# Delta-rule attention with a gated feed-forward on one core: two of four output products moved between the products with the inverse, the inverse stored packed, the next rows normed in halves, four spans to a loop iteration

## The chip, the cores and the metric

One core of a Trainium2 chip. The metric is the device time of one launch in microseconds (us), the median of several runs. PE is TensorE (matmuls), DVE is VectorE, ACT is ScalarE, POOL is GpSimd, SP issues the DMAs. Each engine has its own instruction stream and they meet only at semaphores.

## The reference

For x of shape [2, 4096, 512], in float32:

```
xn = layernorm(x)
q, k = l2norm(heads(xn @ Wq)) / sqrt(32), l2norm(heads(xn @ Wk))       16 heads of 32
v = heads(silu(xn @ Wv));  beta = sigmoid(xn @ Wb)
per head, for each token t:  S += k_t (beta_t (v_t - S^T k_t))^T ;  o_t = S^T q_t
attn = rmsnorm(o) * o_norm_weight @ Wo
ffn = (silu(xn @ fp8(gate_w) * gate_scale) * (xn @ fp8(up_w) * up_scale)) @ fp8(down_w) * down_scale
out = x + attn + ffn
```

## The kernel before

A span is 256 tokens of each of the two batch rows, 512 token rows in four tiles of 128. The 16 spans run one after another, since the states S (a 32 by 32 matrix for each batch row and head) pass from one to the next. `two_spans(it)` on each engine holds two of them (`for par in range(2)`). It is written out once for the first two spans and once as the body of a loop (`Fori(1, SPANS // 2)`, lines 503 to 505), which comes round again before spans 4, 6, 8, 10, 12 and 14, counted from 0: six times. The order on each engine is written by hand, and semaphores count upwards over the whole program.

One span, on PE:

- Thirteen projections (`project`, line 380) of 12 matmuls each, 8 for beta. A factor is split in two 16-bit parts, so each product is three matmuls. Job numbers (line 25) name them: K, Q, B, V. Between them stand the grams (`gram(g)`, g 0 to 7): for chunks of 32 tokens, k^T k and k^T q, as 32 by 32 products in float32. The profile counts 64 matmuls to a `gram` (each float32 product is two).
- Four output products (`project_out`, line 321), 12 matmuls each, with the o of the span before. Its parts `o_hi` and `o_lo` lie in the last four slots of `f_hi` and `f_lo`. DVE adds the results to the residual `xs` (`add_out`, line 1049).
- 24 gate and up products (`gate_up`, lines 390 and 391), 8 matmuls each. ACT takes silu (`silu_gate`), DVE multiplies (`fuse_tile`, line 1013), and each of the 12 tiles is split (`high_part` on ACT, `low_part` on DVE, line 1003).
- Eight groups of products with the inverse (lines 441 to 452; 64 matmuls each in the profile, written `T<-kpv,mt`). Their stationary operand is `tt`, in the memory of `mt`: the transposed inverse of a unit triangular 32 by 32 matrix for each chunk and head. DVE and ACT read the results (`read_w`, line 1042; `copy_u`, line 605).
- The chain over 8 chunks (lines 473 to 501): two blocks of 64 small matmuls a chunk with DVE steps between them (lines 1093 to 1115). In the waits stand pieces of the four down products (`down`, lines 461 and 462) and the transposes of the next span's rows (`transpose_xn`, line 311).

DVE computes the inverse by forward substitution, 62 dependent operations (`row_products`, `off_rows`, lines 1020 and 1027), and does other work between them at places given by tables (lines 43 to 46): `V_AT`, `OUT_AT`, `VK_AT`, `FUSE_AT`, each an operation number to an index. `t_transposed(s)` (line 1037) stores a half of the result transposed into `tt`, with 32 elements of 4 bytes between neighbours it writes:

```
tt = mt[:, :].rearrange("p (n t) -> p n t", t=CHUNK)
nc.vector.transpose(tt[:, 32 * s:32 * s + 32, :].rearrange("p n t -> p t n"), t_prob[:, s])
```

The inverse can start once both halves of the grams are read (`read_grams(s)`, lines 956 to 963). The first four groups of products wait for `tt_ready` of half 0, the last four for half 1.

The next span's rows: SP loads both batch rows when y of the span before last is stored, and that waits for all four `add_out`. DVE takes the statistics of four tiles (line 744) between the last `read_w`, aggregates (line 1103) in chunk 0 of the chain, POOL takes the root (line 726), DVE applies (line 747) in chunks 1 and 2, and PE transposes in chunks 2 to 5. POOL also clears the matrix `at` (line 717), runs the Newton steps for the norms (line 683) and adds the down products (`add_down`, line 732).

## Time and profile before

| | before |
|---|---|
| median of 3 runs | 2594.55 us (2590.03 to 2601.16) |
| the profiled execution, its own time | 2598.04 us |
| its span, first to last instruction | 2596.3 us |
| PE busy | 2290.9 us, 88% |
| DVE busy | 1932.2 us, 74% |
| ACT busy | 661.6 us, 25% |
| POOL busy | 315.2 us, 12% |
| granted PE clock, mean | 0.980 |
| DMA | 54.56 MB, of it 5.47 MB instructions on queue 8 |

In the page a row of a timeline gives the start, the duration, the engine, the line, the operation with its tiles, how many were merged, and in brackets how long the engine had been idle before it and what ended that. "issue" there means that nothing in the profile held the engine. A dense matmul of 512 columns shows 0.38 us, but they follow one another every 0.216 us. One span of the 16 lasts some 152 us.

### The profile page before, as it was taken

The numbers are of one execution on the slowest core, as the hardware profiler recorded it, in microseconds if no ns is written. First come the engines' busy times: TensorE is split into PE (matmuls) and PEld (weight loads), VectorE is DVE, ScalarE is ACT, GpSimd is POOL, SyncE is SP. The second block draws the span as 40 slices with busy tenths as digits, with TensorE's granted clock in tenths as the row PEclk, the third lists the DMA queues.
The fourth block names the chain that finished last, engine by engine and source line by source line (L and its number), as shares of the span: only waits on it lengthen the run. The fifth ranks groups of instructions, "written<-read, shape, count | busy, mean of one in ns | idle before, by whom it ended". The sixth has DMA issues, their size and how long they took to land.

```text
span 2596.3 us, 92717 instructions
## 1 busy us (share of the span) xinstructions
PE 2290.9 (88%) x40736; PEld 1286.9 (50%) x40992; DVE 1932.2 (74%) x3291; ACT 661.6 (25%) x1110; POOL 315.2 (12%) x528
## 2 busy tenths in 40 slices
PE   0198999989899998989989899998989899898996
PEld 0045545455554545455454555545554454545543
DVE  7986685958768596776959587695967769496785
ACT  2123222213222222222222222222222222122221
POOL 4510101001010100102010010201001020100200
PEclk9999999999999999999999999999999999999998
DMA  5100010000001000000000000010100100000010
GB/s 170 61 18 2 3 34 4 33 3 19 18 3 34 3 34 3 17 20 3 34 4 34 3 13 24 3 34 3 34 3 3 34 3 34 4 34 3 2 34 18
DMA packets 27184, 54.56 MB, mean 21 GB/s; under 512 B 5152, under 2 KB 5152, under 8 KB 26784
## 3 DMA queue, kind: packets, MB, share of 16 engines
q1 hardware_dynamic: 26784, 48.55, 5.5%
q8 instruction: 334, 5.47, 0.9%
q14 instruction: 66, 0.54, 0.1%
HBM read 31.76 MB, written 16.78 MB: 19 GB/s over the span
## 4 chain that ended last, share of the span: by engine, by line
PE 88%; issue 6%; DVE 4%; DMA 0%; ACT 0%; POOL 0%; SPq 0%; DVEq 0%
PE D L380 21%; PE T L306 21%; PE D L391 13%; PE D L390 13%; PE D L462 8%; PE D L321 7%; PE D L461 4%; PE D L311 1%; DVE kq L227 1%; DVE at L781 0%; DVE f_lo L780 0%; DVE w_lo L822 0%; DVE stats L744 0%; DVE wgu L233 0%; DVE kq L1042 0%
## 5 line engine op out<-in xcount | busy, mean ns | idle before, releaser
L390 PE MATMUL D<-xt_hi,wgu 128*128 128x512 f16 x1536 | 582.1, 379 | 0.0
L391 PE MATMUL D<-xt_lo,wgu 128*128 128x512 f16 x1536 | 582.1, 379 | 0.0
L462 PE MATMUL D<-wd,f_lo 128*128 128x512 bf16 x768 | 297.0, 387 | 43.1 <-issue 43.1
L380 PE MATMUL D<-xt_hi,w_hi 128*128 128x512 f16 x832 | 319.3, 384 | 12.9 <-issue 12.9
L380 PE MATMUL D<-xt_lo,w_hi 128*128 128x512 f16 x832 | 318.4, 383 | 0.0
L380 PE MATMUL D<-xt_hi,w_lo 128*128 128x512 f16 x768 | 293.9, 383 | 0.0
L598 ACT ACTIVATE sg<-D,gs 128x512 f32<-128x512 f32 x192 | 132.0, 687 | 573.6 <-PE D L391 573.6
L1027 DVE TENSOR_TENSOR at<-at,outer_v 128x62 f32<-128x62 f32 (+15 forms) x496 | 259.3, 523 | 12.1
L1020 DVE TENSOR_TENSOR outer_v<-mt,at 128x62 f32<-128x62 f32 (+15 forms) x496 | 258.2, 521 | 11.6
L391 PEld LDWEIGHTS D<-xt_lo,wgu 128*128 128x128 f16 x1536 | 150.3, 98 | 181.2
L390 PEld LDWEIGHTS D<-xt_hi,wgu 128*128 128x128 f16 x1536 | 150.3, 98 | 181.2
L1113 DVE STREAM_TRANSPOSE outer_p<-T 128x256 f32<-128x256 f32 x128 | 57.6, 450 | 193.4 <-PE T L306 193.4
L461 PE MATMUL D<-wd,f_hi 128*128 128x512 bf16 x512 | 198.2, 387 | 0.0
L306 PE MATMUL T<-kpv,mt 32*32 32x64 f32 x8192 | 136.3, 222 | 67.5 <-issue 67.5
L306 PE MATMUL T<-kq,state 32*32 32x64 f32 x8192 | 155.3, 221 | 24.7 <-ACT kpv L605 18.9
L306 PEld LDWEIGHTS T<-kq,state 32*32 32x32 f32 x8192 | 130.0, 108 | 79.0 <-issue 78.7
L306 PEld LDWEIGHTS T<-kpv,mt 32*32 32x32 f32 x8192 | 126.7, 110 | 81.0 <-issue 81.0
L726 POOL TENSOR_TENSOR rstd<-var_e,neg_half 128x4 f32<-128x4 f32 x16 | 16.4, 1026 | 1222.9 <-DVE var_e L1105 1222.9
L1093 DVE STREAM_TRANSPOSE outer_v<-T 128x256 f32<-128x256 f32 x128 | 57.6, 450 | 143.0 <-PE T L306 143.0
L306 PE MATMUL T<-kpv 32*32 32x64 f32 x8192 | 148.2, 219 | 3.4 <-issue 2.7
L732 POOL TENSOR_TENSOR xs<-xs,fuse 128x512 f32<-128x512 f32 x64 | 81.1, 1267 | 575.8 <-DVE fuse L1087 575.8
L306 PEld LDWEIGHTS T<-kpv 32*32 32x32 f32 x8192 | 125.4, 107 | 46.1 <-issue 45.9
(153 smaller groups left out, 3314.0 us busy)
## 6 DMA issues: line engine op xcount, KB each, us to landing
xs<-_attn_hidden_states_dram SPq DMA_DIRECT2D x34, 512.0 KB, 4.2
out_dram<-xs SPq DMA_DIRECT2D x32, 512.0 KB, 3.3
f_hi<-in_L_ffn_down_w_dram SPq DMA_DIRECT2D x4, 768.0 KB, 4.5
kq<-in_L_ffn_gate_w_dram SPq DMA_DIRECT2D x3, 768.0 KB, 4.4
f_hi<-in_L_ffn_up_w_dram SPq DMA_DIRECT2D x2, 768.0 KB, 6.2
kq<-in_L_ffn_up_w_dram SPq DMA_DIRECT2D x2, 768.0 KB, 6.6
qt<-in_L_attn_Wq_dram SPq DMA_DIRECT2D x1, 1024.0 KB, 8.1
kpv<-in_L_attn_Wk_dram SPq DMA_DIRECT2D x1, 1024.0 KB, 10.4
```

The costliest lines, as they stand in the source:

```text
L306: last = nc.tensor.matmul(out[s], lhs[s], rhs[s], start=start, stop=True, skip_group_check=shared)
L321: ins = nc.tensor.matmul(D[bank][:, :], o_part[:, m, j * P:(j + 1) * P], w[:, m, :], start=n == 0, stop=n == 3 * MS - 1)
L380: last = nc.tensor.matmul(D[bank][:, :], w[:, k, cols], xp[:, k, :], start=n == 0, stop=n == len(parts) * KT_ - 1)
L390: nc.tensor.matmul(D[bank][:, :], wgu[:, k, c:c + P], xt_hi[:, k, :], start=k == 0, stop=False)
L391: last = nc.tensor.matmul(D[bank][:, :], wgu[:, k, c:c + P], xt_lo[:, k, :], start=False, stop=k == KT_ - 1)
L461: nc.tensor.matmul(D[bank][:, :], f_hi[:, ic, j * P:(j + 1) * P], wd[:, ic, :], start=ic == 0, stop=False)
L462: last = nc.tensor.matmul(D[bank][:, :], f_lo[:, ic, j * P:(j + 1) * P], wd[:, ic, :], start=False, stop=ic == IC - 1)
L598: nc.scalar.activation(sg[:, ic % 2, :], D[bank_of(gate_up_job(2 * ic))][:, :], ACT.Silu, scale=gs[:, ic:ic + 1]).then_inc(sg_ready, 1)
L732: nc.gpsimd.tensor_tensor(xs[:, par, j, :], xs[:, par, j, :], fuse[:, j % 2, :], ALU.add).then_inc(acc_ready, 1)
L1020: solved[0] = step(nc.vector.tensor_tensor(products(j), m_prob[:, :, j, j + 1:].unsqueeze(3).to_broadcast(shape), t_prob[:, :, j, 0:j + 1] ...
L1027: solved[0] = step(nc.vector.tensor_tensor(rest, rest, products(j), ALU.subtract))
L1093: nc.vector.transpose(blocks(outer_v), chain_banks(c)[:, :, :, 0, :]).then_inc(ws_read, 1)
```

## The change

- PE: output products 0 and 1 stay ahead of the gate and up products. Products 2 and 3 are cut in halves of 6 matmuls, and one half follows every second of the eight groups with the inverse. A gram pair is separated by a projection, and four matmuls of job 9 stand ahead of grams 6 and 7. The beta projection comes sixth instead of third.
- The inverse's transpose is packed: DVE writes it contiguously, and PE reads its stationary operand with a step of 32 elements.
- o: DVE writes the normed o into `at`, and the two 16-bit parts lie in the memory of `qt`. The last span's parts stay in `f_hi` and `f_lo`. POOL clears `at` after `o_low` instead of at the span's start, so writing beta on the diagonal became a step of its own (`set_diagonal`).
- DVE: all 12 `fuse_tile` stand between the operations of the inverse; `add_out` 2 and 3 follow during the products with the inverse.
- Rows of the next span: each batch row is loaded, measured, aggregated and applied by itself, with a semaphore each.
- Loops: `some_spans(it)` holds four spans, written out once and looped three times, so it comes round twice.

```diff
+TURNS = 4
-JOB_K, JOB_B, JOB_Q, JOB_V, JOB_WO, JOB_GU, JOB_DN = (0, 3, 5, 7), 2, (1, 4, 6, 8), (9, 10, 11, 12), 13, 17, 41
+JOB_K, JOB_B, JOB_Q, JOB_V, JOB_WO, JOB_GU, JOB_DN = (0, 2, 4, 7), 5, (1, 3, 6, 8), (9, 10, 11, 12), (13, 14, 39, 40), 15, 41
-XT_AT = {2: 0, 3: 1, 4: 2, 5: 3}
+XT_AT = {2: 0, 3: 1, 5: 2, 6: 3}
-V_AT = {0: 0, 4: 1, 9: 2, 13: 3}
-OUT_AT = {17: 0, 20: 1, 22: 2, 25: 3}
-VK_AT = 23
-FUSE_AT = {27: 0, 31: 1, 34: 2, 37: 3, 40: 4, 43: 5, 46: 6, 50: 7, 54: 8, 60: 9}
+V_AT = {0: 0, 2: 1, 7: 2, 12: 3}
+OUT_AT = {16: 0, 18: 1}
+VK_AT = 18
+FUSE_AT = {20: 0, 24: 1, 27: 2, 30: 3, 33: 4, 36: 5, 39: 6, 42: 7, 45: 8, 49: 9, 53: 10, 58: 11}
+STATS_AT, AGGREGATE_AT, APPLY_AT = {2: 1}, {0: 0, 3: 1}, {1: 0, 4: 1}
...
-        tt = mt[:, :].rearrange("p (n t) -> p n t", t=CHUNK)
+        tt = mt[:, :].rearrange("p (g t n) -> p g t n", g=2, t=CHUNK)
-        o_hi, o_lo = f_hi[:, IC - MS:, :], f_lo[:, IC - MS:, :]
+        o_half = o_wide.bitcast(F16)
+        o_hi, o_lo = (o_half[:, i * MS * TOK:(i + 1) * MS * TOK].rearrange("p (m n) -> p m n", m=MS) for i in range(2))
+        last_hi, last_lo = f_hi[:, IC - MS:, :], f_lo[:, IC - MS:, :]
+        o_normed = at[:, :]
...
-                    sp.wait_ge(wo_added, at_span(it, par, TILES, 2 * TILES))
...
+                    for b in range(BATCH):
+                        sp.wait_ge(wo_added, at_span(it, par, TILES, TILES + 2 * b + 2, turns=2))
+                        sp.nop(nofuse=True)
+                        store_y(it * 2 + par, par, b)
+                        sp.wait_ge(y_stored, at_span(it, par, 32, 16 * b + 16, turns=2))
+                        sp.nop(nofuse=True)
+                        load_x(it * 2 + (par + 2), par, b)
...
-                    project(8)
                     gram(4)
                     gram(5)
+                    project(8)
+                    project(9, end=4)
                     gram(6)
                     gram(7)
-                    for job in range(9, PROJECTIONS):
+                    project(9, first=4)
+                    for job in range(10, PROJECTIONS):
                         project(job)
 
                     pe.wait_ge(olo_ready, since(1, 1))
-                    for j in range(TILES):
-                        project_out(j, take(JOB_WO + j))
+                    for j in range(2):
+                        project_out(j, take(JOB_WO[j]))
...
-                            last = quads(T[g % 4][:, 64 * n:64 * n + 64], tt[:, pc, :], kpv[:, 1:3, pc * DH:(pc + 1) * DH])
+                            last = quads(T[g % 4][:, 64 * n:64 * n + 64], tt[:, pc // 32, :, pc % 32], kpv[:, 1:3, pc * DH:(pc + 1) * DH])
                         last.then_inc(tiled_done, 1)
+                        if g % 2:
+                            j, half = 2 + g // 4, g // 2 % 2
+                            bank = bank_of(JOB_WO[j]) if half else take(JOB_WO[j])
+                            project_out(j, bank, groups=range(2 * half, 2 * half + 2))
...
-            with pe.Fori(1, SPANS // 2) as it:
-                two_spans(it)
+            with pe.Fori(1, SPANS // TURNS) as it:
+                some_spans(it)
...
-                    pool.wait_ge(xt_lo_ready, since(TILES, TILES))
+                    o_norm(it, turn, step, after_last)
+                    pool.wait_ge(olo_ready, since(1, 1))
                     pool.nop(nofuse=True)
                     nc.gpsimd.memset(t_flat, 0.0).then_inc(zero_ready, 1)
-                    o_norm(it, par, step, after_last)
...
-                        nc.vector.transpose(tt[:, 32 * s:32 * s + 32, :].rearrange("p n t -> p t n"), t_prob[:, s]).then_inc(tt_ready, 1)
+                        nc.vector.transpose(tt[:, s], t_prob[:, s]).then_inc(tt_ready, 1)
...
                     t_transposed(0)
-                    fuse_tile(10)
                     t_transposed(1)
-                    fuse_tile(11)
-
-                    dve.wait_ge(x_loaded, since(32, 64))
-                    dve.nop(nofuse=True)
+
                     for g in range(8):
                         read_w(g)
                         if g == 1:
                             low_part(IC - 1)
-                        if g > 3:
-                            step(layer_norm_stats(g - 4, 1 - par))
+                        if g == 4:
+                            add_out(2)
+                    read_statistics(0)
+                    add_out(3)
...
+                        if c in AGGREGATE_AT:
+                            aggregate(AGGREGATE_AT[c])
+                        if c in APPLY_AT:
+                            apply_norm(APPLY_AT[c])
...
+                        if c in STATS_AT:
+                            read_statistics(STATS_AT[c])
```

New functions on DVE: `read_statistics(b)` waits for `x_loaded[b]` and takes the statistics of tiles 2b and 2b+1, `aggregate(b)` and `apply_norm(b)` do the rest for them.

How the instructions of PE move, at the products with the inverse. Before, first the last gate and up products, then all eight groups (256 products are 512 matmuls in the profile), then the chain:

```order
L390 MATMUL D<-xt_hi,wgu 128x512
L391 MATMUL D<-xt_lo,wgu 128x512
L306 MATMUL T<-kpv,mt 32x64 x256
L306 MATMUL T<-kq,state 32x64 x32
L461 MATMUL D<-wd,f_hi 128x512
L462 MATMUL D<-wd,f_lo 128x512
```

The same place with the change (the line of `quads` is now 314, that of `project_out` 329):

```order
L401 MATMUL D<-xt_lo,wgu 128x512
L314 MATMUL T<-kpv,mt 32x64 x64
L329 MATMUL D<-wo_hi,qt 128x512 x2
L329 MATMUL D<-wo_lo,qt 128x512
L329 MATMUL D<-wo_hi,qt 128x512 x2
L329 MATMUL D<-wo_lo,qt 128x512
L314 MATMUL T<-kpv,mt 32x64 x64
L329 MATMUL D<-wo_hi,qt 128x512 x2
L329 MATMUL D<-wo_lo,qt 128x512
```

Six dense matmuls now follow every two groups, 24 in all, and they are gone from the place ahead of the gate and up products.

On DVE, the end of the inverse before. Line 1037 is `t_transposed`, 1003 and 1013 are `low_part` and `fuse_tile`:

```order
L1020 TENSOR_TENSOR outer_v<-mt,at 128x62
L1027 TENSOR_TENSOR at<-at,outer_v 128x2x31
L1037 STREAM_TRANSPOSE mt<-at 128x32x32
L1003 TENSOR_TENSOR f_lo<-fuse,f_hi 128x512
L1013 SCALAR_TENSOR_TENSOR fuse<-D,usf,sg 128x512
L1037 STREAM_TRANSPOSE mt<-at 128x32x32
L1003 TENSOR_TENSOR f_lo<-fuse,f_hi 128x512
L1013 SCALAR_TENSOR_TENSOR fuse<-D,usf,sg 128x512
L1042 STREAM_TRANSPOSE kq<-T 128x8x32 x2
```

And with the change (1071 is `t_transposed`, 1076 `read_w`, 1083 `add_out`, 765 the statistics):

```order
L1054 TENSOR_TENSOR outer_v<-mt,at 128x62
L1061 TENSOR_TENSOR at<-at,outer_v 128x2x31
L1071 STREAM_TRANSPOSE mt<-at 128x1024 x2
L1076 STREAM_TRANSPOSE kq<-T 128x8x32 x2
L1037 TENSOR_TENSOR f_lo<-fuse,f_hi 128x512
L1076 STREAM_TRANSPOSE kq<-T 128x8x32 x3
L1083 SCALAR_TENSOR_TENSOR xs<-D,w_inv,xs 128x512
L1076 STREAM_TRANSPOSE kq<-T 128x8x32 x3
L765 BN_STATS stats<-xs 128x6 x2
L1083 SCALAR_TENSOR_TENSOR xs<-D,w_inv,xs 128x512
```

Both transposes follow the inverse at once and write 1024 elements in a row; tiles 10 and 11 have moved ahead of them, output adds 2 and 3 behind.

## Rows read from the trace of the kernel before

**Rows 1.** The page, part 4: the chain of work that ended last, by engine.
```profile
PE 88%; issue 6%; DVE 4%; DMA 0%; ACT 0%; POOL 0%; SPq 0%; DVEq 0%
```
**Rows 2.** Windows, span 6: length; PE, PEld, DVE, ACT, POOL busy; clock; DMA.
```profile
1086.00:1138.00 52.00, 52.00 (x243) 23.52 (x241) 49.52 (x80) 14.69 (x24) 0.00 (x0) 1.00 0.13 41
1138.00:1153.00 15.00, 10.09 (x527) 9.19 (x528) 8.03 (x16) 3.58 (x9) 0.00 (x0) 0.89 0.02 5
1153.00:1196.00 43.00, 38.72 (x1120) 25.36 (x1128) 21.42 (x48) 5.57 (x13) 4.82 (x4) 1.00 0.01 3
```
**Rows 3.** Groups of PE over the run: busy, mean ns, idle before and its releaser.
```profile
L380 PE MATMUL D<-xt_hi,w_hi 128*128 128x512 f16 x832 | 319.3, 384 | 12.9 <-issue 12.9
...
L306 PE MATMUL T<-kpv,mt 32*32 32x64 f32 x8192 | 136.3, 222 | 67.5 <-issue 67.5
...
L306 PE MATMUL T<-kq 32*32 32x64 f32 x8192 | 129.5, 215 | 19.9 <-issue 19.9
```
**Rows 4.** Timeline of PE, span 4: products with the inverse, then the chain's start.
```profile
832.42 2.56 PE L306 MATMUL T<-kpv,mt 32*32 32x64 f32 x168
836.60 1.98 PE L306 MATMUL T<-kpv,mt 32*32 32x64 f32 x126 [1.62 <-issue]
840.53 1.98 PE L306 MATMUL T<-kpv,mt 32*32 32x64 f32 x126 [1.95 <-issue]
...
847.23 2.33 PE L306 MATMUL T<-kq,state 32*32 32x64 f32 x64 [1.15 <-ACT kpv L605]
```
**Rows 5.** Timeline of PE, span 6, at the same place.
```profile
1138.26 2.56 PE L306 MATMUL T<-kpv,mt 32*32 32x64 f32 x168
...
1146.10 3.59 PE L306 MATMUL T<-kpv,mt 32*32 32x64 f32 x126 [1.95 <-issue]
...
1152.83 0.71 PE L306 MATMUL T<-kq,state 32*32 32x64 f32 x34 [1.19 <-ACT kpv L605]
```
**Rows 6.** Timeline of PE, span 7, at the same place.
```profile
1290.31 3.88 PE L306 MATMUL T<-kpv,mt 32*32 32x64 f32 x261
...
1302.71 0.21 PE L306 MATMUL T<-kq,state 32*32 32x64 f32 x1 [1.20 <-ACT kpv L605]
```
**Rows 7.** Timeline of PE: first matmul of span 6, some after; one of span 10.
```profile
1042.59 0.39 PE L380 MATMUL D<-xt_hi,w_hi 128*128 128x512 f16 x1 [2.16 <-issue]
...
1044.05 0.63 PE L380 MATMUL D<-xt_hi,w_hi 128*128 128x512 f16 x1
1044.47 0.63 PE L380 MATMUL D<-xt_lo,w_hi 128*128 128x512 f16 x1
...
1652.53 0.63 PE L380 MATMUL D<-xt_hi,w_hi 128*128 128x512 f16 x1
```
**Rows 8.** Timeline of PE, span 6: grams 4 to 7.
```profile
1075.20 0.87 PE L306 MATMUL T<-kq 32*32 32x64 f32 x46 [1.11 <-issue]
```
**Rows 9.** Timeline of DVE, span 6: from the grams' reading to the inverse's transposes.
```profile
1076.12 1.25 DVE L956 STREAM_TRANSPOSE mt<-T 128x1024 f32<-128x1024 f32 x1 [2.17 <-PE T L306]
...
1089.42 0.74 DVE L1049 SCALAR_TENSOR_TENSOR xs<-D,w_inv,xs 128x512 f32<-128x512 f32 x1
1090.08 0.58 DVE L1027 TENSOR_TENSOR at<-at,outer_v 128x414 f32<-128x414 f32 x1
...
1133.39 1.98 DVE L1037 STREAM_TRANSPOSE mt<-at 128x1024 f32<-128x1024 f32 x1
1135.22 0.67 DVE L1003 TENSOR_TENSOR f_lo<-fuse,f_hi 128x512 f16<-128x512 f32 x1
...
1136.46 1.94 DVE L1037 STREAM_TRANSPOSE mt<-at 128x1024 f32<-128x1024 f32 x1
```
**Rows 10.** Timeline of DVE, span 6: a step of the chain in chunk 3.
```profile
1170.68 0.45 DVE L1093 STREAM_TRANSPOSE outer_v<-T 128x256 f32<-128x256 f32 x1 [0.32 <-PE T L306]
```
**Rows 11.** Timeline of SP, span 6: y stored, x loaded.
```profile
1100.02 0.97 SPq L279 DMA_DIRECT2D out_dram<-xs  x2
1105.55 0.97 SPq L275 DMA_DIRECT2D xs<-_attn_hidden_states_dram  x2
```

233 lines of the change are left out of this document (124 added, 109 removed).

## The prediction

> **What bounds the kernel now.** I read the chain of work that ended last first: PE holds 88% of it and time without a releaser 6% [rows 1]. So PE's own stream sets the end, and a change is worth what it takes out of that stream, or out of its gaps. Next the windows of one span in the middle of the run [rows 2]. In the dense middle (52 us) PE is busy all the time and DVE for 49.5 us. In the chain (43 us) PE is busy for 38.7. In the 15 us with the products of the inverse PE is busy for only 10.1, and its clock is 0.89. The groups of PE say what these holes are [rows 3]: 67.5 us in all before the products with the inverse, 19.9 us before the grams, 12.9 us before first projections, nearly all under "issue", with no semaphore named.
>
> The timeline shows what they look like [rows 4]. From 832.42 us 168 small matmuls run in 2.56 us, then PE stands still, then come 126 in 1.98 us, and again. The blocks begin at 836.60 and 840.53, 3.93 us apart, and 126 matmuls with their weight loads are 252 instructions. I read this as the instruction stream: small matmuls use instructions faster than they arrive, some 256 per 3.9 us. Dense matmuls need 2 instructions per 0.216 us, seven times fewer than arrive. So a small matmul stage is worth filling with dense work, and that is what the change does. The products with the inverse last 14.8 us in span 4, 14.6 in span 6, 12.4 in span 7, from first product to the chain's start [rows 4 to 6].
>
> **The change, part by part.** Costs are per middle span; 15 spans count, since the first is set by its setup as well.
>
> Loop: PE stands still 12.9 us in six first projections [rows 3], 2.16 us in one of them [rows 7]; these are the six times when the loop comes round. Two remain, four go: 4 × 2.15 = 8.6 us. After that stop the matmuls of span 6 follow each other every 0.42 us, with durations of 0.63, a clock of half speed, for 8 matmuls: 1.7 us more. Three of the six loop heads show it (spans 6, 10 and 14 [rows 7]), so of four removed I take off two: 3.4 us.
>
> Grams: the stop of 1.11 us [rows 8], 19.9 / 16 = 1.2 us a span [rows 3], goes, since a projection and four more matmuls now stand between. Those four matmuls are ahead of gram 7 instead of behind it: 4 × 0.216 = 0.9 us later. Of the 0.3 us left I count 0.2, since a little of the stop may stay: 3.0 us over 15 spans.
>
> Start of the products with the inverse. This is the term on which most depends, since PE and DVE are now equally long here. From DVE's reading of gram 7 (1076.12) PE reaches the products at 1138.26, after 62.1 us, and DVE has the first transposed half at 1133.39 + 1.98 = 1135.37, after 59.3 [rows 5, 9]. PE loses two output products (24 × 0.216 = 5.2 us) and the four matmuls from that stretch and would arrive after 56.1. DVE: two output adds go behind, 0.66 us each from start to start [rows 9], 1.3; the first transpose becomes contiguous, and for it I take the other transpose of 1024 elements, 1.25 us [rows 9], so 0.7 less; tiles 10 and 11 come ahead of it, each with its low part 1.24 us (1135.22 to 1136.46 [rows 9]), 2.5 more; and of the 2.5 us that DVE is idle in this stretch, waiting for PE [rows 2], I count 0.5 as gone. That gives 59.3 − 1.3 − 0.7 + 2.5 − 0.5 = 59.3. With the semaphore's way of 0.3 us PE starts after 59.6, 2.5 us earlier than before, not 5.2 + 0.9. DVE becomes the bound of this stretch, and PE waits about 3.5 us in a place where it never waited: −2.5 × 15 = −37.5 us.
>
> Length of that stage. Its work is 512 × 0.0140 us (2.56 less a tail of 0.2, over 168 [rows 4]) = 7.2, plus 24 × 0.216 = 5.2, plus some 1.0 for eight changes between small and dense, plus the 1.2 us for ACT's last copy [rows 4]: 14.6 us if instructions never lack. By instructions: 1024 + 48 less the 336 of the first block is 2.9 blocks of 3.93 us, behind a first arrival after 4.2 us: the last block arrives after 12 us and takes 1 to 3 more. Work and arrivals don't overlap perfectly. Before it was 13.9 us on average over rows 4 to 6; I take 15.6, so +1.7 × 15 = +25.5 us. Lower end: 13.9, nothing more; upper end 18, if both delays add. The Trainium skill (Runtime: NRT & Kernel Launch, Instruction fetch mechanics) holds that crossing from one block of instructions to the next is mostly hidden. By that the stage would take its 14.6 us of work, the sum would be 15 us lower; the stops of 1.62 and 1.95 us per 252 instructions [rows 4] contradict it, and they decide.
>
> Clock there. In span 6 126 matmuls take 3.59 us instead of 1.98 [rows 5], so half speed also comes after stops of 1.4 to 1.9 us. It then costs little, since instructions were lacking anyway. Now PE is idle for 3.5 us before the stage, and work fills the stage: 3.4 us at half speed would cost up to 1.7. I take +0.4 × 15 = +6 us; ends 0 and +1.7 a span.
>
> Chain. Statistics of the second batch row (2 × 0.65 us) come in chunk 2, beside a low part and a down product's reading, before DVE's step of chunk 3, for which DVE had only 0.32 us to wait [rows 10]. So that step is about 0.9 us late, and PE has a down piece and one transpose (0.5) less to cover it: +0.2 a span, +3 us. In return chunk 0 and 2 lose the aggregation and one apply, which were covered.
>
> At nothing I cost: tanh behind the o copy on ACT (busy 25%); POOL's clearing, 1.8 us, now after `o_low`, which has several us of grams and sums on DVE before `set_diagonal`; the beta projection's place; o's parts in `qt` (same sizes). Loads: the second row's store can start only after output add 3, now at the chain's start instead of at 1099.8. From there store and load took 1100.02 to some 1111 us, 11 us [rows 11]. The statistics of that row come some 16 us into the chain, so it is covered with 4 to 5 us to spare.
>
> Sum: −8.6 − 3.4 − 3.0 − 37.5 + 25.5 + 6 + 3 = −18.0 us. On the profiled execution, 2598.0, that is 2580.0; it was 3.5 us above the median of the runs, so I expect a median of 2576.6 us.
>
> **The rivals.**
>
> A, the gain is whole. Instructions arrive in time and the clock stays up: stage +0, clock +0. −8.6 − 3.4 − 3.0 − 37.5 + 3 = −49.5, so 2545 us. For it: the dense pieces give each pair of groups 1.3 us in which hardly an instruction is used. Against: 3.9 us per 256 instructions remains, and 1072 are needed.
>
> B, nothing is gained in the spans. If the write step is not what makes the transposes take 1.98 us, they stay, +0.7 a span, and the stage comes to 15.9: per span −2.5 + 0.7 + 2.0 + 0.4 + 0.2 − 0.2 = +0.6, so +9 against −12 for the loops: 2592 us. Against: the other 1024-element transpose takes 1.25 us [rows 9] though it reads with a step. The change then doesn't do what it says.
>
> C, slower: the packed inverse moves the step from DVE's write to PE's weight load, which now reads 32 elements 128 bytes apart. No row has such a load. From below the price is zero, if loads stay behind the matmuls before them. From above it is DVE's: (1.98 − 1.25) / 1024 = 0.7 ns per element, 23 ns per load of 32. Four row groups load side by side, 64 × 2 loads follow one another in each: 3.0 us a span, in a stage now filled with work: −18 + 45 − 3 = +24, so 2619 us. It decides from about 16 ns a load on (2.1 us a span, which turns −18 into +13). For it: small matmuls at half clock take twice the time (3.59 against 1.98 us [rows 5]), so the array and not the issue sets their pace, and a slower load may show. Against: for half of each pair the array streams 64 columns, behind which a load can hide. The Trainium skill (Advanced Engine Details and Errata, SBUF Cachelines) speaks against the change here: lines are 16 bytes, and a new line with each access costs. By that the transposes get faster and the loads slower, as the 1.98 against 1.25 us bears out for DVE.
>
> D, slower: PE's idle 3.5 us puts every stage at half speed for some 6.8 us, twice as long as in rows 5. Its work is then 3.4 us longer, of which lacking instructions hide some 0.8: +2.6 a span for the +0.4, so −18 + 2.2 × 15 = +15, 2610 us. It decides from 2.5 us a span on.
>
> **How the numbers follow.** About 0.5%, 13 us, is what a measurement can tell. Chances: my forecast 0.34, A 0.15, B 0.26, C 0.16, D 0.09. Faster by over 0.5% (below 2581.6): forecast and A, 0.49. Within: B, 0.26. Slower (over 2607.5): C and D, 0.25. Range: from below A, with the stage's start a further 0.3 us earlier a span, 2540, up to C with a little of D, 2624. My own case alone: 2562 to 2590.
>
> **What would show it.** PE's group of first projections waits 2 times, some 4 us. The grams' 19.9 us nearly vanish. Before the first product with the inverse PE is idle some 3 to 4 us, released by DVE's transpose: right for the start term. That transpose takes 1.2 to 1.3 us: else B. A group of 64 of these products takes clearly over 1.1 us at full clock: C. The output matmuls between them show 0.63 us: D. Stage from first product to the chain some 15.6 us. If PE is not idle before it, or the stage takes as long as before, my two largest terms are wrong.

## The result: slower by a third of a per cent, and the profile after

| | before | after |
|---|---|---|
| median of the runs, us | 2594.21 (18 runs, 2588.11 to 2604.66) | 2602.31 (18 runs, 2596.98 to 2609.03) |
| ratio | | 1.0033, 95% interval 1.0023 to 1.0044 |
| span of the profiled execution, us | 2596.3 | 2600.4 |

The forecast was 2576.6 us. The time lies in its range and within 0.5% of before, but the change moved it the other way. The change cost some 8 us.

All times below that are given by span come from the timeline of PE, cut at five points of each span: first projection, first output product, end of the last gate/up product, first product with the inverse, start of the chain. Summed over the 16 spans, after against before (in brackets what one span takes, before and after; for the stage the mean of spans 1 to 14):

| part of the span | after less before, us |
|---|---|
| projections and grams | +2.8 |
| output products, gate and up | −82.9 (51.8, then 46.6) |
| PE's wait ahead of the products with the inverse | +67.1 (0.1, then 4.1 to 4.4) |
| stage of the products with the inverse | +34.3 (13.70, then 16.04) |
| chain, and the gap to the next span | −17.4 |
| sum | +3.9 |

The two profiled executions differ by 4.1 us, so the table holds nearly all of it. Span 0 is an exception in the stage: it took 19.2 us there before and 15.6 after.

First the windows of span 12 of the changed kernel, cut at its own edges; they answer to [rows 2]. Columns: length, busy time of PE, weight loads, DVE, ACT and POOL, the granted clock, the share and rate of the DMAs.

```profile
1996.00:2047.60 51.60, 51.60 (x240) 23.29 (x238) 48.87 (x84) 16.60 (x27) 0.00 (x0) 1.00 0.06 21
2047.60:2052.00 4.40, 0.20 (x5) 0.06 (x5) 4.11 (x9) 0.63 (x1) 0.00 (x0) 0.91 0.00 0
2052.00:2067.70 15.70, 14.97 (x536) 10.94 (x536) 6.63 (x13) 3.07 (x8) 0.00 (x0) 0.92 0.02 4
2067.70:2110.00 42.30, 40.62 (x1134) 25.20 (x1134) 23.00 (x51) 5.08 (x11) 5.18 (x5) 1.00 0.09 28
```

There is a row that before did not have: 4.4 us in which PE does next to nothing and DVE works. In the stage behind it PE is busy for 14.97 of 15.70 us, where it was busy for 10.09 of 15.00. The filling worked; the 4.2 us ahead of it ate what it brought.

The groups of PE answer to [rows 3], with the weight loads of the same products:

```profile
L390 PE MATMUL D<-xt_hi,w_hi 128*128 128x512 f16 x832 | 319.5, 384 | 6.3 <-issue 6.3
...
L314 PE MATMUL T<-kpv,mt 32*32 32x64 f32 x8192 | 159.9, 238 | 69.1 <-DVE mt L1071 50.4 <-issue 18.3
L314 PE MATMUL T<-kq 32*32 32x64 f32 x8192 | 131.9, 215 | 16.1 <-issue 15.3 <-ACT kq L575 0.8
...
L314 PEld LDWEIGHTS T<-kpv,mt 32*32 32x32 f32 x8192 | 148.9, 141 | 99.0 <-issue 98.7
```

The idle time ahead of the products with the inverse is as large as before (69.1 against 67.5 us), but another kind. It was stops inside the stage. Now 50.4 us are one wait of 4.2 us for DVE's transpose of the inverse (L1071), named in 12 spans; in the other four the same wait stands under "issue". The grams' stops have not gone, 16.1 against 19.9 us.

The timeline of PE in span 12 answers to [rows 4 to 6]: the products with the inverse between the output products (one row is kept of each of those), and the chain's first group.

```profile
2051.97 3.25 PE L314 MATMUL T<-kpv,mt 32*32 32x64 f32 x128 [4.20 <-DVE mt L1071]
2055.15 0.61 PE L329 MATMUL D<-wo_hi,qt 128*128 128x512 f16 x2
...
2056.55 2.10 PE L314 MATMUL T<-kpv,mt 32*32 32x64 f32 x128
...
2059.97 2.08 PE L314 MATMUL T<-kpv,mt 32*32 32x64 f32 x128
...
2063.39 2.09 PE L314 MATMUL T<-kpv,mt 32*32 32x64 f32 x128
...
2067.71 1.10 PE L314 MATMUL T<-kq,state 32*32 32x64 f32 x64
```

128 small products take 2.1 us at full clock, and 3.25 us behind the wait (3.06 to 3.64 over the 16 spans). Only one stop of 0.73 us is left inside this stage, and the chain starts without the 1.15 us for ACT's copy [rows 4].

DVE in the same place answers to [rows 9]: its last gated tile, the last two rows of the inverse, and both transposes in one row.

```profile
2047.96 0.69 DVE L1037 TENSOR_TENSOR f_lo<-fuse,f_hi 128x512 f16<-128x512 f32 x1
2048.57 0.74 DVE L1047 SCALAR_TENSOR_TENSOR fuse<-D,usf,sg 128x512 f32<-128x512 f32 x1
...
2050.12 0.22 DVE L1061 TENSOR_TENSOR at<-at,outer_v 128x62 f32<-128x62 f32 x1
2050.38 2.37 DVE L1071 STREAM_TRANSPOSE mt<-at 128x1024 f32<-128x1024 f32 x2
```

Two transposes in 2.37 us: the step in the write was indeed what made each take 1.98. But PE is kept waiting until 2051.97.

What DVE itself waits for shows in the chain of work that ended last (start, duration, engine and line), from PE's last gate/up product to the products with the inverse; the stretches under "issue" and the inverse's rows between are left out:

```profile
2047.56 0.23 PE D L401
...
2047.96 0.10 DVE f_lo L1037
...
2048.57 0.74 DVE fuse L1047
...
2050.38 1.26 DVE mt L1071
2051.63 0.34 issue
2051.97 3.25 PE T L314 x128
```

The chain runs along PE to its last gate/up product and only there goes over to DVE: that product belongs to tile 11, and `fuse_tile(11)` waits for it even ahead of tile 10's low part. In all 16 spans DVE starts this low part 0.42 or 0.57 us after the start of that product, after 0.15 us of idling; then follow 2.41 us for the low part, the tile and four operations of the inverse, 1.25 for the transpose and 0.21 or 0.35 of way. That is 4.28 or 4.58 us from the product's start, and explains why the wait hardly varies.

And the grams of span 10, which answer to [rows 8]:

```profile
1675.28 1.88 PE L314 MATMUL T<-kq 32*32 32x64 f32 x118
1678.41 0.38 PE L314 MATMUL T<-kq 32*32 32x64 f32 x10 [1.25 <-issue]
...
1682.28 1.65 PE L314 MATMUL T<-kq 32*32 32x64 f32 x100
1686.10 1.06 PE L314 MATMUL T<-kq 32*32 32x64 f32 x28 [2.17 <-issue]
...
1687.50 0.63 PE L390 MATMUL D<-xt_hi,w_lo 128*128 128x512 f16 x1
```

One stop of 1.1 us had become two, 3.4 us together, with half clock behind them (0.63 us for a projection matmul instead of 0.38). I ask below whether such stops stand where PE's stream of instructions passes from one block of 256 to the next; I call that place an edge. Spans 0, 1, 6, 10 and 14 look like this and take 44.9 to 46.9 us from the first projection to the first output product. The other eleven take 40.9 to 42.6, where before took 42.0 to 43.8 in its spans 1 to 15.

### The profile page after: what moved, and what is told of

Its sections match the earlier page's. It is cut to its first block, busy times and chain, and to the rows that moved or that the text cites. A ratio compares the mean times of both kernels' runs of the same rounds, so it can differ in the third digit from the quotient of the medians.

```text
span 2600.4 us, 92532 instructions
## 1 busy us (share of the span) xinstructions
PE 2354.5 (91%) x40992; PEld 1294.3 (50%) x40992; DVE 1918.8 (74%) x3307; ACT 663.9 (26%) x1110; POOL 325.7 (13%) x544
## 4 chain that ended last, share of the span: by engine, by line
PE 89%; DVE 7%; issue 3%; DMA 0%; POOL 0%; ACT 0%; DVEq 0%; SPq 0%
PE T L314 22%; PE D L390 21%; PE D L401 13%; PE D L400 13%; PE D L329 7%; PE D L477 7%; PE D L478 6%; PE D L319 1%; DVE kq L232 1%; DVE mt L1071 1%; DVE kpv L1154 0%; DVE at L803 0%; DVE f_lo L802 0%; DVE state L1163 0%; DVE w_lo L844 0%
## 5 line engine op out<-in xcount | busy, mean ns | idle before, releaser
L477 PE MATMUL D<-wd,f_hi 128*128 128x512 bf16 x768 | 293.7, 382 | 1.5 <-issue 1.4
L478 PE MATMUL D<-wd,f_lo 128*128 128x512 bf16 x768 | 291.1, 379 | 0.0
L314 PE MATMUL T<-kpv,mt 32*32 32x64 f32 x8192 | 159.9, 238 | 69.1 <-DVE mt L1071 50.4
L748 POOL TENSOR_TENSOR rstd<-var_e,neg_half 128x2 f32<-128x2 f32 x32 | 22.6, 706 | 1486.2 <-DVE var_e L1099 1486.2
L314 PEld LDWEIGHTS T<-kpv,mt 32*32 32x32 f32 x8192 | 148.9, 141 | 99.0 <-issue 98.7
L1076 DVE STREAM_TRANSPOSE kq<-T 128x256 f32<-128x256 f32 x128 | 57.4, 448 | 153.2 <-PE T L314 153.1
L329 PE MATMUL D<-wo_hi,qt 128*128 128x512 f16 x512 | 159.0, 392 | 1.3 <-issue 1.2
L314 PEld LDWEIGHTS T<-kq,state 32*32 32x32 f32 x8192 | 123.4, 105 | 67.3 <-issue 67.2
L314 PE MATMUL T<-kq,state 32*32 32x64 f32 x8192 | 148.0, 216 | 8.2 <-issue 5.1
L314 PEld LDWEIGHTS T<-kpv 32*32 32x32 f32 x8192 | 122.8, 105 | 50.7 <-issue 50.5
```

What stands on the lines that cost most here:

```text
L314: last = nc.tensor.matmul(out[s], lhs[s], rhs[s], start=start, stop=True, skip_group_check=shared)
L329: ins = nc.tensor.matmul(D[bank][:, :], o_part[:, m, j * P:(j + 1) * P], w[:, m, :], start=m == 0 and n == 0, stop=m == MS - 1 and n == 2)
L477: nc.tensor.matmul(D[bank][:, :], f_hi[:, ic, j * P:(j + 1) * P], wd[:, ic, :], start=ic == 0, stop=False)
L478: last = nc.tensor.matmul(D[bank][:, :], f_lo[:, ic, j * P:(j + 1) * P], wd[:, ic, :], start=False, stop=ic == IC - 1)
L1076: nc.vector.transpose(kq[:, 8 * g:8 * g + 8, 0, :], T[g % 4][:, :].rearrange("p (n a d) -> p n a d", n=8, a=2)[:, :, 0, :]).then_inc(w_rea ...
```

## The experiments

Ratios are to runs of before on the same chip, with their 95% intervals. "The changed kernel" is the one above, 1.0033. The traces come from several chips, on which before took 2586.9 to 2594.2 us. Two of them are of the changed kernel with nothing but empty instructions added, and between these three the mean of spans 1 to 14 is 15.96 to 16.17 us for the stage and 42.38 to 42.80 up to the output products: smaller differences than that say nothing.

**Two gated tiles behind the transposes.** If the wait is DVE's, take DVE's work out of its way.

```
-FUSE_AT = {..., 45: 8, 49: 9, 53: 10, 58: 11}
+FUSE_AT = {..., 45: 8, 49: 9}
...
                     t_transposed(0)
+                    fuse_tile(10)
                     t_transposed(1)
+                    fuse_tile(11)
```

> The changed kernel with tiles 10 and 11 of the gated product (each with its low part 1.24 us on DVE) put back behind the first and the second transpose of the inverse, where before had its last tiles. PE waits 4.1 to 4.4 us a span for the first of these transposes. Theory G (DVE's own row of work between the grams and the transposes sets the start of the inverse products): 2.5 us less work stand ahead of the first transpose, so PE's wait falls to about 1.7 us, the stage starts 2.5 us earlier in each span, and, if the stage keeps its 16.0 us, the time falls by 2.5 x 16 = 40 us, to 2562. Rival H (the instruction stream sets the end of the stage, which is where PE's blocks of small products arrive): the wait before the stage shrinks but the stops inside it grow by as much, 16.0 becomes 17.5 to 18.5, and the time falls by 0 to 15 us, 2587 to 2602. Rival I (the low parts are now late for the down products in the chain, or the second group's transpose is late): the stage gets 1.2 us longer by waits for DVE, time 2582.

Measured: 2536.28 us, 0.9803 (0.9782 to 0.9823). PE:

```profile
L314 PE MATMUL T<-kpv,mt 32*32 32x64 f32 x8192 | 143.1, 221 | 33.3 <-DVE mt L1071 17.9 <-issue 14.9
```

Two lines of order on DVE turn a loss of 0.33% into a gain of 2%. G holds and H falls: PE's wait fell from 4.1 to 4.4 us to 1.4 to 1.7, and the stage did not grow but shrank, from 16.04 to 14.82 us on average over spans 1 to 14. The chain of work now goes over from PE to DVE earlier, at tile 9 (at 2000 us in span 12, 8.6 us ahead of the products with the inverse), so tile 11 no longer ties the inverse to PE's last product. The stage starts 3.05 us earlier and is 1.2 us shorter. The second part I had not expected; the products' mean duration fell from 238 to 221 ns, which pointed at the clock. The granted clock in the stage says the same: on average over spans 1 to 14 it was 0.87 in the changed kernel and is 1.00 here. The stage of span 12, against the row above with a clock of 0.92:

```profile
2008.60:2023.80 15.20, 13.89 (x536) 9.91 (x536) 8.99 (x17) 4.11 (x10) 0.00 (x0) 1.00 0.02 5
```

Span 0 goes the other way: its stage takes 22.98 us instead of 15.64. ACT scales the 12 tiles of the down weights once, there, behind its last high part, and its copies of the products wait behind that. With tile 11 later this work starts later, and PE stands still before the third pair of groups:

```profile
222.43 7.44 ACT L632 ACTIVATE wd<-wd,row_inv 128x512 bf16<-128x512 bf16 x12
```

```profile
230.23 2.95 PE L314 MATMUL T<-kpv,mt 32*32 32x64 f32 x99 [4.77 <-issue]
```

All kernels below with tiles 10 and 11 behind the transposes have a long stage in span 0 (19.6 us in the one with all output products in front, 21 to 22 in the others). Against 15 us in the other spans some 6 to 8 us, 0.3%, are left there for an order that scales the weights elsewhere; no run tried it.

**One low part more behind the transpose.** `fuse_tile(9)` no longer starts with tile 8's low part, which now stands ahead of `fuse_tile(10)`.

```
-                            fuse_tile(FUSE_AT[op])
+                            fuse_tile(FUSE_AT[op], low=FUSE_AT[op] != 9)
...
                     t_transposed(0)
+                    low_part(8)
                     fuse_tile(10)
```

> As the kernel that took tiles 10 and 11 behind the transposes of the inverse (0.980 of before), and tile 8's low part (0.6 us on DVE) also goes behind the first transpose instead of ahead of tile 9. PE still waited 1.4 to 1.7 us a span for that transpose. If DVE's row of work is still what sets the start, the wait falls by 0.6 us, and 16 x 0.6 = 10 us come off: 0.976 of before. If the instruction stream now sets the end of the stage, the stage grows by as much, and the ratio stays 0.980.

Measured: 2524.43 us, 0.9769 (0.9742 to 0.9796). The wait fell to 0.7 to 1.1 us, the stage stayed (14.87), and a span lost another 0.85 us, 0.6 of it in the wait. DVE's row of work is still what decides there. The intervals of this ratio and the last overlap; the wait itself does not leave doubt:

```profile
L314 PE MATMUL T<-kpv,mt 32*32 32x64 f32 x8192 | 143.3, 220 | 23.9 <-issue 12.1 <-DVE mt L1071 10.7
```

**The wait filled with matmuls for nothing.** The changed kernel, with

```
                     pe.wait_ge(vk_ready, since(1, 1))
+                    pe.wait_ge(m_ready, since(2, 2))
+                    pe.wait_ge(p_ready, since(2, 2))
+                    for n in range(16):
+                        nc.tensor.matmul(T[0][:, :], wgu[:, 0, 0:P], xt_hi[:, 0, :], start=True, stop=True)
                     for g in range(8):
```

> The changed kernel with 16 matmuls of 128x512, whose result nothing reads, ahead of the first product with the inverse (3.5 us of work in the 4.1 to 4.4 us in which PE waits there). Theory K (the wait before the stage is what lowers the clock at its start, and the low clock makes the stage 16.0 us instead of the 14.8 that it takes in the kernel whose wait is 1.4 to 1.7 us): the clock stays up, the first products take 216 ns and the stage 14.8 to 15.0 us; the stage's mean falls by 1.0 to 1.2 us a span, up to 19 us in all. Rival L (the stage is longer because instructions lack, and the wait has nothing to do with it): the stage stays at 16.0 us or gets longer, since 32 more instructions pass. The 32 instructions a span also move the edges in the grams, so the whole time may differ by some long spans; the stage is read by itself.

Measured: 2588.35 us, 0.9980 (0.9966 to 0.9994), so work that nobody needs makes the changed kernel some 14 us faster. The timeline, the 16 matmuls and the first two groups behind them:

```profile
1425.13 3.62 PE L456 MATMUL T<-xt_hi,wgu 128*128 128x512 f16 x16
1429.30 2.09 PE L314 MATMUL T<-kpv,mt 32*32 32x64 f32 x128 [0.55 <-DVE mt L1075]
...
1432.72 2.09 PE L314 MATMUL T<-kpv,mt 32*32 32x64 f32 x128
```

The start is no earlier (4.0 to 4.2 us from the last gate/up product to the first product with the inverse), but the first 128 products take 2.09 us in every span where they took 3.06 to 3.64, and the stage is 15.06 us on average instead of 16.04, at a granted clock of 1.00 instead of 0.87. K holds. The wait costs twice: itself, and 1 us of low clock behind it. Not all of the gain need be the clock, since the 32 instructions a span also move the stops in the grams.

**The inverse unpacked.** Layout and transposes as before, all else changed.

```
-tt = mt[:, :].rearrange("p (g t n) -> p g t n", g=2, t=CHUNK)
+tt = mt[:, :].rearrange("p (n t) -> p n t", t=CHUNK)
...
-    last = quads(T[g % 4][:, 64 * n:64 * n + 64], tt[:, pc // 32, :, pc % 32], ...)
+    last = quads(T[g % 4][:, 64 * n:64 * n + 64], tt[:, pc, :], ...)
...
-    nc.vector.transpose(tt[:, s], t_prob[:, s])
+    nc.vector.transpose(tt[:, 32 * s:32 * s + 32, :].rearrange("p n t -> p t n"), t_prob[:, s])
```

> The changed kernel with the transposed inverse laid out as before: DVE writes it with a step, PE loads it contiguously. Theory: DVE's two transposes together take 3.9 us again instead of 2.4, 0.7 us later for the first half, so PE's wait before the inverse products is 0.7 us longer, 4.9 us, and the stage starts 0.7 us later; each weight load in it takes 110 ns instead of 141, worth 0.4 us a span in bursts where 128 products take 2.09 us. Net +0.3 to +0.7 a span, 5 to 11 us slower than the changed kernel, 2607 to 2613. Rival C of the prediction in a small form (the strided loads cost more than the bursts show): the stage is 1 us or more shorter, and the time 2595 or less.

Measured: 2608.45 us, 1.0074 (1.0052 to 1.0095), 0.4% or 10.6 us over the changed kernel. DVE, then PE, from the end of the transposes on:

```profile
2056.58 3.67 DVE L1071 STREAM_TRANSPOSE mt<-at 128x1024 f32<-128x1024 f32 x2
```

```profile
2058.84 3.64 PE L314 MATMUL T<-kpv,mt 32*32 32x64 f32 x128 [4.87 <-DVE mt L1071]
...
2064.46 2.00 PE L314 MATMUL T<-kpv,mt 32*32 32x64 f32 x128
```

The wait is 0.66 us longer a span, which is the 10.6 us. At full clock 128 products take 2.00 us with contiguous loads and 2.09 with strided ones: 0.09 × 4 = 0.4 us a span is what the strided loads can cost by these rows, and the stage's mean (16.20 here, 16.04 in the changed kernel) shows nothing of it. Packing is worth what it takes from DVE. The Trainium skill (Advanced Engine Details and Errata, SBUF Cachelines) says that a different 16-byte line with each access costs. That is borne out for DVE, 3.67 against 2.37 us for the two transposes. For PE the weight loads do get longer (141 ns in the changed kernel, 120 here), but nearly all of it lies beside matmuls.

**All output products in front again.** The changed kernel with `project_out` for all four ahead of the gate and up products, and DVE's tables of before (the last two tiles behind the transposes).

```
-JOB_..., JOB_WO, JOB_GU, ... = ..., (13, 14, 39, 40), 15, ...
+JOB_..., JOB_WO, JOB_GU, ... = ..., (13, 14, 15, 16), 17, ...
...
-                    for j in range(2):
+                    for j in range(TILES):
                         project_out(j, take(JOB_WO[j]))
...
-                        if g % 2:
-                            ...
```

> The changed kernel with all four output products ahead of the dense middle again, and DVE's output adds and gated tiles at the places that they had in the kernel before; kept are the packed inverse, four spans to a loop iteration, the norming in halves and the interleaved grams. It tells what the pieces are worth on their own. Before had 52 us of dense middle, no wait, and 13.7 us of inverse products. If the pieces themselves bring nothing but what DVE's order gives back, this kernel has a wait of 0 to 0.5 us, a stage of 13.7, and is some 7 us (loop heads) faster than before: 0.997. Against the kernel with tiles 10 and 11 behind the transposes (0.980) that would make the pieces worth 1.7%, 44 us, or 2.8 us a span out of the 5.2 us of matmuls that they move. If it comes out near 0.985 instead, the pieces are worth little and the gain of that kernel came from the packing and the loop.

Measured: 2598.51 us, 1.0054 (1.0030 to 1.0077). No wait (0.1 us), a stage of 14.53 us, and 0.5% slower than before where I expected 0.3% faster. Without the pieces the loop, the packing, the norming and the interleaved grams together bring nothing, and cost some 14 us. Against the first kernel of this section (0.9803) the pieces are worth 2.5% once DVE's order lets them: the start of the stage is 3.8 us earlier (94.48 against 90.67 from the span's start), and the stage with two output products in it takes 14.82 us against 14.53 without. Of 5.2 us of matmuls moved into the stage, 0.3 us show there. I expected 13.7 us for this stage. The stops inside it are those of before (4.1 us a span in both) and so is the last wait for ACT (1.2); it is the 512 products that are busy for 9.3 us instead of 8.4:

```profile
989.69 2.08 PE L314 MATMUL T<-kpv,mt 32*32 32x64 f32 x126 [1.54 <-issue]
```

126 of them take 2.08 us with strided loads and took 1.98 with contiguous ones [rows 4], 0.4 us for 512. So here, with no dense work between, the strided loads do cost. A granted clock of 0.94 instead of 0.95 gives perhaps 0.2 more; the rest is open.

**Shifting PE's stream.** Two kernels have 24 and 64 empty instructions on PE ahead of the first span.

```
             pe.wait_ge(ffn_ready, 1)
+            for _ in range(24):
+                pe.nop(nofuse=True)
```

> The changed kernel with 24 empty instructions on PE ahead of the first span, so that everything behind them stands 24 places later in PE's stream. Theory E (the stops between grams come where the stream crosses from one block of 256 instructions to the next, and hurt only in those copies of the span in which such an edge falls into grams 4 to 7 at a bad place): the five long spans (0, 1, 6, 10, 14, with 46.5 us from start to the output products where the others have 41.0) change. By my count of the instructions the copies stand at other places and none or one (that of spans 5, 9 and 13) is then bad: the time falls by 5.3 x 5 = 26 us, to 2576, or by 5.3 x 2 = 11, to 2592, if the copy of spans 5, 9, 13 becomes bad. Rival F (the stops belong to the order of the work, for instance to what DVE and ACT do beside the grams): 24 empty instructions, under 1 us once, change nothing; the same five spans are long and the time is 2602.

> The same with 64 empty instructions. Theory E: the copy of spans 5, 9 and 13 then stands where that of spans 6, 10, 14 stood, so spans 5, 9, 13 get the 5.3 us and spans 0, 1, 6, 10, 14 lose them: 2 x 5.3 = 11 us faster than the changed kernel, 2592, and the long spans are others. Rival F: no change in time, and the same spans are long.

Measured: 2596.03 us, 1.0027 (1.0011 to 1.0043), and 2599.36 us, 1.0038 (1.0022 to 1.0055). The same five spans are long. That looks like F, but the trace says more. I numbered all records of PE in it from the start: matmuls, weight loads and the waits and register operations of its sequencer. In the changed kernel the two stops of span 1 stand before numbers 6337 and 6593, those of span 6 before 32193 and 32449: 256 apart each, and 101 × 256 from one span to the other. With 24 or 64 empty instructions ahead all four numbers are the same. The empty instructions themselves leave no record, so the stops stand before the very same matmuls. Either edges don't matter, or empty instructions don't shift them. These two runs decide nothing by themselves.

**The same with real instructions.**

```
                 pe.wait_ge(sq_ready, i + 1)
+                if i == len(SQUARE_ORDER) - 1:
+                    for c in range(32):
+                        nc.tensor.matmul(T[0][:, 200 + c:201 + c], squares[i % 2][:, (c % IC) * P:(c % IC + 1) * P], ones[:, :],
+                                         start=True, stop=True)
```

> The changed kernel with 32 tiny matmuls (128x1, results unused) with their weight loads among those of the setup, 64 recorded instructions ahead of the first span, at once behind its setup. The 24 and 64 empty instructions moved no stop by a single recorded instruction, so they stood nowhere in the stream that the stops count; these do. Theory E (edges of blocks of 256 instructions): counted in recorded instructions, an edge now falls 26 + 64 instructions before and so on in each copy, so that the copy of spans 5, 9 and 13 (gram 4 began 14 instructions past such a place after the shift, as that of span 1 did before it) becomes long, 45 to 47 us up to the output products, and spans 0, 1, 6, 10, 14 short, 41 to 42. Time: 3 long spans for 5, about 2 x 5 = 10 us less than the changed kernel, ratio to before 0.999. Rival F (spans 1, 6, 10, 14 are long for what else happens in them or for the time at which they come): the same spans are long as without the tiny matmuls, ratio 1.003.

Measured: 2592.52 us, 1.0023 (1.0008 to 1.0038). PE's grams 4 to 7, first in span 5, then in span 6:

```profile
905.80 1.88 PE L314 MATMUL T<-kq 32*32 32x64 f32 x119
909.21 0.32 PE L314 MATMUL T<-kq 32*32 32x64 f32 x9 [1.53 <-issue]
...
913.02 1.65 PE L314 MATMUL T<-kq 32*32 32x64 f32 x101
916.57 0.63 PE L314 MATMUL T<-kq 32*32 32x64 f32 x27 [1.90 <-issue]
...
1062.36 2.00 PE L314 MATMUL T<-kq 32*32 32x64 f32 x128
...
1067.84 2.00 PE L314 MATMUL T<-kq 32*32 32x64 f32 x128
```

Theory E holds. 64 recorded instructions in the setup, a microsecond of work, and the two stops of span 6 are gone and stand in span 5, after nearly the same counts (118, 10, 100, 28 in span 10 of the changed kernel; 119, 9, 101, 27 here). Spans 0, 5, 9 and 13 are long now (49.5, 46.6, 44.6 and 44.9 us), spans 1, 6, 10 and 14 take 40.9 to 41.0. The stops stand before numbers with the same remainder by 256 as before the shift (27073 and 6337 both leave 193). In time the gain is small where I expected 10 us: three long spans and a longer span 0 take the place of five, and two of the chains have become long (46.4 and 48.2 us in spans 7 and 11). The interval overlaps that of the changed kernel.

The Trainium skill (Runtime: NRT & Kernel Launch, Instruction fetch mechanics) says that crossing a block's edge is mostly hidden. In dense stretches it is (PE is busy for all of the 51.6 us in the first window above); between two grams that stand 12 or 16 dense matmuls apart, it costs 1.53 and 1.90 us in these rows, and whether it does hangs on where the edge falls.

**The last four grams behind one another.** Projection ahead of gram 4, four matmuls behind gram 7.

```
                     project(7)
+                    project(8)
                     gram(4)
                     gram(5)
-                    project(8)
-                    project(9, end=4)
                     gram(6)
                     gram(7)
-                    project(9, first=4)
-                    for job in range(10, PROJECTIONS):
+                    for job in range(9, PROJECTIONS):
```

> The changed kernel with the last four grams behind one another again, and the projection and the four matmuls that stood between grams 5 and 6 around them (the projection ahead of gram 4, the four matmuls behind gram 7). By the prediction's term for the grams each span gets its stop of 1.1 us back and gram 7 is read some 0.3 us later, +1 us a span, 16 us slower than the changed kernel, 2610 on the scale on which that took 2602. By theory E the interleaving is what makes five spans 4 to 5 us long and saves 1 us in the other eleven: undone, 11 x 1 us are lost and 5 x 3 us are won, and the time is within 5 us of the changed kernel.

Measured: 2589.73 us, 1.0017 (1.0002 to 1.0032), if anything better than the changed kernel. Every fourth span takes 40.8 to 40.9 us up to the output products and nearly all others 42.1 to 42.7; none of spans 1 to 15 is long. Against this the interleaving gives 1.2 to 1.7 us in seven spans and 0.6 in span 0, takes 2.6 to 4.8 in spans 1, 6, 10 and 14, and 0.5 to 1.4 in the other four. With four spans to an iteration it gains nothing, where my term for it was −3 us.

**Dense work spread evenly, in the grams and then in the stage too.** From the second kernel of this section (0.9769):

```
                     gram(4)
+                    project(8, end=6)
                     gram(5)
-                    project(8)
-                    project(9, end=4)
+                    project(8, first=6)
                     gram(6)
+                    project(9, end=4)
                     gram(7)
```

and, in the second of them, besides that:

```
-                        if g % 2:
-                            j, half = 2 + g // 4, g // 2 % 2
-                            bank = bank_of(JOB_WO[j]) if half else take(JOB_WO[j])
-                            project_out(j, bank, groups=range(2 * half, 2 * half + 2))
+                        j, m = 2 + g // 4, g % 4
+                        bank = bank_of(JOB_WO[j]) if m else take(JOB_WO[j])
+                        project_out(j, bank, groups=range(m, m + 1))
```

> The kernel with tiles 10, 11 and the low part of 8 behind the transposes (0.977 of before), and the dense matmuls among the last four grams spread evenly: half a projection (6 matmuls, 1.3 us) between grams 4 and 5 and between 5 and 6, the four matmuls between 6 and 7. Nothing is added and gram 7 has the same matmuls ahead of it. Theory E: one gram uses about 140 instructions and 6 dense matmuls then give 1.3 us for the next to arrive, so that no span stops for long wherever the edges lie; spans 0, 1, 6, 10 and 14 come down from 44.4 to 46.6 to about 41.3, 20 us in all: 0.969. Rival: each change from small to dense work costs as much as is saved (two changes more a span), and the ratio stays at 0.977.

> The last kernel, and in the stage of the inverse products the two output products are cut finer: 3 matmuls (0.65 us) behind every group of 64 small products instead of 6 behind every second. If the stage is short of instructions after a pair of groups (stops of over 1 us inside it, 12.1 us in all before these products), it gets 0.5 us shorter a span: 8 us, 0.966. If eight changes more a span cost 0.1 us each, it is 0.8 us longer: 0.974.

Measured: 2536.62 us, 0.9787 (0.9766 to 0.9809), and 2547.91 us, 0.9827 (0.9804 to 0.9850). Both rivals hold. The long spans did shrink, to 43.2 to 43.9 us (46.1 in span 0), but the good ones rose from 41.0 to 42.2. In the stage the finer cut made 14.96 into 15.66 us, and there the two intervals hardly touch. Grams 4, 5 and 6 of span 6 of the first of them, and gram 6 of span 7, a good one:

```profile
1041.46 1.09 PE L314 MATMUL T<-kq 32*32 32x64 f32 x64
...
1043.89 1.14 PE L314 MATMUL T<-kq 32*32 32x64 f32 x64
...
1047.17 1.10 PE L314 MATMUL T<-kq 32*32 32x64 f32 x64 [0.73 <-issue]
...
1195.93 1.09 PE L314 MATMUL T<-kq 32*32 32x64 f32 x64 [0.73 <-issue]
```

A stop of 0.73 us is there in good and long spans alike; in span 7 of the kernel that this one is made from there was none. The rest of the 1.2 us is the changes between small and dense work. In span 7 the first small matmul starts 0.31 us after the last dense one, 0.09 more than the 0.216 between dense ones, and the next dense one 1.03 us after the first small one, 0.13 more than 64 × 0.0140. So a group of small matmuls among dense ones costs some 0.2 us, an estimate from these starts, and there are two groups more a span. In the stage there are four more, and it grew by 0.7.

**The loop alone undone.**

```
-TURNS = 4
+TURNS = 2
```

> The changed kernel with two spans to a loop iteration, as before had it; everything else as in the change. By the prediction's terms for the loop the four loop heads that come back cost 2.15 us each and 3.4 us together for the low clock behind two of them: 12 us slower than the changed kernel, ratio to before 1.008. By what the trace of the changed kernel shows (stops before first projections 12.9 us before, 6.3 after) it is 7 us slower at least, 1.006. Theory E adds that the copies of the span stand elsewhere in the stream, so that the long spans (45 us and more up to the output products) are others than 1, 6, 10, 14, and by their number 5 us a piece come or go.

Measured: 2606.61 us, 1.0050 (1.0032 to 1.0067), some 4 us over the changed kernel, with intervals that overlap. First projections:

```profile
L390 PE MATMUL D<-xt_hi,w_hi 128*128 128x512 f16 x832 | 318.1, 382 | 12.7 <-issue 12.7
```

Six stops of 1.90 to 2.41 us, 12.7 us; in the changed kernel there are two such stops, 2.53 and 2.03 us, and three small ones elsewhere. So four heads are 8.1 us, as forecast (8.6). But with two spans to an iteration only spans 0 and 1 are long, so projections and grams are 1.2 us a span shorter, and the chain with its gaps 1.2 us longer. Summed over the 16 spans, projections and grams take 669.3 us here and 686.7 in the changed kernel; the chain with its gaps 738.0 and 718.6. So most of what the longer loop takes out of the one part it puts into the other, since the edges came to stand elsewhere.

**Three last kernels,** all from the second kernel of this section (0.9769): with the edit of the 32 tiny matmuls; with that of the grams behind one another; and with the tiny matmuls and

```
-TURNS = 4
+TURNS = 8
```

> The kernel with tiles 10, 11 and the low part of 8 behind the transposes (0.977 of before), with the 32 tiny matmuls of the setup. Both effects are thought to be independent. Theory E: long spans are 5, 9 and 13 instead of 0, 1, 6, 10 and 14, 2 fewer at 3.5 to 5 us each, 7 to 10 us off: 0.973 to 0.974. Rival (the stage of the inverse products and the chain have their own bad places, which move too and give back what the grams win): 0.976 to 0.978, with other stage lengths than 14.87 on average.

> The same kernel (0.977), without the tiny matmuls and with the last four grams behind one another. In the changed kernel that was worth 4 us (1.0017 against 1.0033), since it makes all spans 42.3 us up to the output products instead of eleven at 41.0 and five at 45 to 47. If that adds to the early transposes: 0.975. Gram 7 comes some 0.3 us later in a good span, and DVE's row sets the start of the inverse products, so it may also be nothing: 0.977.

> The kernel with early transposes and tiny matmuls, and eight spans to a loop iteration: one pass of the loop is left where there were three. From four spans to two the stops ahead of first projections went from 6.3 to 12.7 us, 1.1 us for each of 6 heads or 2.1 for each visible one; the two heads that go are worth 2 to 4.5 us, and half clock behind them up to 1.7 each. Expected 3 to 8 us under the first kernel of this group, if the edges of the blocks, which move with the loop, leave the number of long spans at three; with five long spans it is 0 to 5 us slower instead.

Measured: 2537.78 us, 0.9787 (0.9760 to 0.9813); 2526.78 us, 0.9752 (0.9724 to 0.9779); 2523.39 us, 0.9732 (0.9707 to 0.9757). The first is the rival: no gain. Its grams are 0.24 us a span shorter, its stage 0.17 and its chain 0.16 longer, all within what repeats show; what is clear is that span 0 takes 50.5 us up to its output products instead of 45.8, and that the chains of spans 7 and 11 are long again (46.3 us). The second is no different from its parent within the intervals. The third is the fastest of this study, 14 us under the first of the three where I expected 3 to 8; its first projections show no stop at all:

```profile
L394 PE MATMUL D<-xt_hi,w_hi 128*128 128x512 f16 x832 | 318.5, 383 | 0.0
```

Not even the one head that remains shows one, which I can't explain. Its lead over 0.9769 and 0.9752 is within their intervals.

## Why the prediction was wrong, point by point

**Loop heads, −8.6 us: right.** Four of six visible stops went, 12.9 us of [rows 3] became 4.6 for the two that stayed. What I left out is that doubling the loop's body moves every edge of 256 instructions behind it.

**Clock at loop heads, −3.4 us: right in size.** Eight projection matmuls of 0.63 us stood behind three of six heads, and stand behind one of two (span 8). They count in the part of projections and grams.

**Chain, +3.0 us: too pessimistic.** Chain and gaps came to −17.4 us against a forecast of −8.6 + 3.0 = −5.6. With the loop undone the chain and its gaps go back to 44.31 us, before's 44.24, so the surplus came with the loop as well. The norming in halves shows no price.

**Grams, −3.0 us: failed.** The term is what was left of a stop of 1.2 us a span, 18 us, that was to go. Projections and grams should have become 18 + 3.4 = 21.4 us shorter, and became 2.8 longer: the largest miss of all. The step "goes, since a projection and four more matmuls now stand between" took the stop for a matter of how much small work stands together. It is also a matter of where the block's edge falls, and in four spans of 16 it fell where two stops of 1.3 to 2.2 us took the place of one of 1.1 (span 0, long before the change too, has two of 0.8 and 1.4). The rows for this were in hand: blocks of 252 instructions every 3.9 us [rows 4]. I used them for one stage and not for the other. A shift by 64 recorded instructions moved the long spans to other copies, which shows it. In the good spans the stop did go (42.3 to 41.0 us), and with the loop undone this part is 14.6 us shorter than in before. So it is the two changes together that failed: the longer loop put the edges where the interleaved grams suffer from them. What the longer loop adds here (17.4 us) nearly cancels what it takes from the chain with its gaps (19.4), and of the 12.0 us forecast for the loop some 4 are measured.

**Start of the products with the inverse, −37.5 us: PE does wait, but the path was wrong.** PE waits 4.1 to 4.4 us where I said 3.5, and from DVE's reading of gram 7 to the first product it takes 60.1 us in span 3 and 60.4 in spans 7 and 12, some 1.8 less than the 62.1 of [rows 5, 9] instead of 2.5 less. The transposes take what I took for them. What failed is to add up DVE's work from the grams on as one row, as if it could run ahead of PE, with 0.5 us of its idle time "gone". DVE's idle time between reading gram 7 and the end of the first transpose is 2.9 to 3.1 us in spans 3, 7 and 12, and was 2.8 to 2.9: nothing went. Tile 11 needs PE's last gate/up product, and with the tile ahead of the transpose the inverse can't be handed over before that product, then 2.4 us of DVE's work, the transpose and the way. My own figure for PE's arrival, 56.1 us, and the 4.2 us of the wait give the 60.3. Together with the four matmuls that were moved ahead of gram 7, the stage starts 1.0 us earlier after the first output product, where my terms gave 1.6, and 0.8 us earlier after the span's start (94.49 to 93.72), where they gave 2.7. That it is tile 11 that ties the hand-over to PE is read from the code and the chain of work; no run moved tile 11 alone.

**Stage +25.5 and clock +6, 31.5 us together: right, at 34.3,** with the split wrong. The stage without the low clock is 14.8 to 15.1 us (the kernels with a short or a filled wait), not 15.6, and the low clock costs 1.0 to 1.2 us a span, not 0.4. Half speed was D's mechanism, at less than half of its price (2.6). The 34.3 us are the net of span 0, 3.6 us shorter, and the other 15, 37.8 longer.

**The rivals.** A fell: filling the stage costs something, and the wait. B fell, the transposes take 1.2 us each. C fell, some 0.4 us a span instead of 3.0. D is in, small; its sign, output matmuls of 0.63 us, does not show in span 12 (0.38 each), only the first 128 small ones are slow. None of them was what happened. The missing case was the plain one that DVE's own order of work takes the gain, and I had it in my terms: I wrote that tiles 10 and 11 "come ahead of it, 2.5 more". I priced the two tiles and did not ask what the change would be without them. It would have been 2%, as the first experiment shows.

**In the sum:** projections and grams came out 24 us worse than forecast (−21.4, then +2.8). From the first output product to the stage it was 8 us worse: −2.5 + 0.9 = −1.6 us a span, −24.0, then −82.9 + 67.1 = −15.8. The stage was 3 us worse (+31.5, then +34.3). Chain and loop heads were 12 us better (−5.6, then −17.4). Cut like this my terms give −19.5 (1.5 of it because I took 0.2 for 0.3 us a span in the grams), and −19.5 + 24.2 + 8.2 + 2.8 − 11.8 = +3.9.

One reading of before was also wrong, without harm. Of the 6% under "issue" in the chain of waits [rows 1], 43.1 us stand before `f_lo` matmuls of the down products:

```profile
L462 PE MATMUL D<-wd,f_lo 128*128 128x512 bf16 x768 | 297.0, 387 | 43.1 <-issue 43.1
...
L461 PE MATMUL D<-wd,f_hi 128*128 128x512 bf16 x512 | 198.2, 387 | 0.0
```

Only 512 of 768 `f_hi` matmuls are in that trace, but all 768 of their weight loads: the holes are 256 records that are missing, 0.17 us each, and no idle time. So PE was busier in before than the 88% of the page.

## What to carry to other kernels

When work is moved off the engine that bounds a stretch, look at once at the engine that is next, and take everything from in front of its hand-over that nobody needs yet: here two tiles and a low part behind a transpose instead of ahead of it made a kernel that is 2.3% faster out of one that was 0.3% slower. Ask of every piece in that row what it waits for itself: a tile that needs the last product of the bounding engine makes the hand-over wait for that product too. A wait of some 4 us costs itself and then a microsecond of low clock; if it can't be removed, matmuls for nothing in it can pay. And where small matmuls use up instructions faster than they arrive, compare spans of a kernel with each other before blaming a change: 2 to 4% of a span hang on where block edges fall, and 64 recorded instructions more in the setup moved them.

## What the runs showed of the hardware that I had not expected

- Stops between small matmuls stand 256 records of PE apart (sequencer's included), or multiples of it, in the spans written out ahead of the loop and in its first pass, and 15 more per pass after that (remainders 193, 208, 223 in spans 6, 10 and 14). Thirty-two tiny matmuls with their loads, ahead of it all, moved them; 24 and 64 empty instructions did not move them by one. Whether these ever entered the stream, no run shows.
- The same code costs 40.9 or 46.9 us up to the output products, and which copies are the slow ones changes with the place of the edge.
- Behind an idle 4.2 us, 128 small products took 3.06 to 3.64 us instead of 2.09; behind 1.5 us idle they took 2.08 to 2.26, and behind 3.6 us of useless matmuls and 0.55 us idle 2.09.
- 32x32 weight loads with a step of 128 bytes between elements: 2.09 us for 128 products against 2.00, while the same step in DVE's write made two transposes take 3.67 us instead of 2.37.
